# A graph layer on sorted edges: block bounds found by search and histogram, edge attributes kept column by column, one-hots shared with GpSimd

## The reference, cut to what matters

```python
def _L0_gnn_ref(x, edge_index, edge_attr, Wf1, bf1, Wf2, bf2, Wn1, bn1, Wn2, bn2):
    past, future = (edge_index[0], edge_index[1])
    x_p = x[past]
    x_f = x[future]
    flow_fwd = jnp.concatenate([x_f, x_p, edge_attr], axis=1)
    flow_bwd = jnp.concatenate([x_p, x_f, edge_attr], axis=1)
    flow_total_in = jnp.concatenate([flow_fwd, flow_bwd], axis=0)
    flow_processed = _mlp(flow_total_in, Wf1, bf1, Wf2, bf2)
    dest = jnp.concatenate([future, past], axis=0)
    flow_total = jax.ops.segment_sum(flow_processed, dest, num_segments=x.shape[0])
    return _mlp(flow_total, Wn1, bn1, Wn2, bn2)

def _L1_gnn_ref(x, edge_index):
    row, col = (edge_index[0], edge_index[1])
    return jax.ops.segment_sum(x[col], row, num_segments=x.shape[0])

h = jnp.maximum(_layernorm(x, axis=-1), 0.0)
x = x + _L0_gnn_ref(h, edge_index, edge_attr_16, ...)
h = jnp.maximum(_layernorm(x, axis=-1), 0.0)
x = x + _L1_gnn_ref(h, edge_index)
```

## Time and profile before

| | us |
|---|---|
| runs: median of 3 | 7755.75 |
| runs: lowest, highest | 7750.64, 7782.26 |
| profiled execution: span from first to last instruction | 7771.8 |
| busy: PE, weight loads, POOL, DVE, ACT | 5666.4, 4762.1, 4917.2, 3545.9, 1215.0 |

### The profile page before, as it was taken

One profiled execution on the slowest core, in us unless ns is written; L12 is line 12 of the kernel. 1 busy time (PEld: TensorE's weight loads), 2 busy tenths in 40 slices (PEclk: granted clock), 3 DMA queues, 4 the chain that ended last, 5 costly groups with the idle time before them and its releaser, 6 DMA issues.

```text
span 7771.8 us, 126735 instructions
## 1 busy us (share of the span) xinstructions
PE 5666.4 (73%) x26327; PEld 4762.1 (61%) x26328; DVE 3545.9 (46%) x15179; ACT 1215.0 (16%) x4039; POOL 4917.2 (63%) x4924
## 2 busy tenths in 40 slices
PE   2199999999999899999899998999943333333334
PEld 2077777777777777777777776888833333333334
DVE  8944444444444444444444444888833232232233
ACT  3211111111111111111111112333310000000000
POOL 0077777777777777777777775000037777777774
PEclk8566666666666766666666666555565555555555
DMA  5011111111111111111111112333211111111111
GB/s 130 5 41 41 41 41 41 41 40 41 41 40 40 40 40 41 40 40 40 41 40 40 40 40 52 68 70 70 60 16 14 14 14 14 14 14 14 14 14 17
DMA packets 1104013, 292.10 MB, mean 38 GB/s; under 512 B 1010042, under 2 KB 1052328, under 8 KB 1103553
## 3 DMA queue, kind: packets, MB, share of 16 engines
q1 hardware_dynamic: 947294, 102.88, 10.0%
q0 software_dynamic: 156672, 188.71, 9.8%
HBM read 226.56 MB, written 82.32 MB: 40 GB/s over the span
## 4 chain that ended last, share of the span: by engine, by line
POOL 54%; issue 27%; PE 11%; DVE 5%; DMA 2%; DVEq 1%; POOLq 0%; ACT 0%; ACTq 0%; SPq 0%
POOL t L518 19%; POOL records L486 18%; POOL g L476 17%; PE bank L782 4%; PE bank L732 1%; PE bank L731 1%; DVE acc L1007 1%; DVE oht L1076 1%; PE bank L730 1%; DVE ohd L1076 1%; PE bank L837 1%; DVEq L280 1%; DMA g<-t_rows,rec_i 1%; PE bank L758 0%; DMA t<-records 0%
## 5 line engine op out<-in xcount | busy, mean ns | idle before, releaser
L518 POOL DMA_INDIRECT t<-h_rows,didx x1568 | 1496.0, 954 | 1403.8 <-DMA didx<-records 925.9
L486 POOL DMA_INDIRECT records<-rec,pos x1664 | 1759.3, 1057 | 626.7 <-issue 451.3
L476 POOL DMA_INDIRECT g<-t_rows,rec_i x1664 | 1656.3, 995 | 756.0 <-issue 492.0
L837 PE MATMUL bank<-t,ohd 128*128 x1664 | 376.1, 402 | 1323.0 <-DMA t<-h_rows,didx 1323.0
L1016 DVE TENSOR_TENSOR prod<-bank,q_row 128x392 f32<-128x392 f32 x416 | 235.8, 567 | 2214.2 <-PE bank L747 2037.1
L730 PE MATMUL bank<-g,ident 128*128 128x128 f32 x3328 | 908.5, 367 | 379.3 <-DMA g<-t_rows,rec_i 378.2
L837 PEld LDWEIGHTS bank<-t,ohd 128*128 128x128 f32 x1664 | 362.9, 330 | 1335.8 <-issue 1335.8
L732 PE MATMUL bank<-t,oht 128*128 x3328 | 1113.4, 429 | 0.0
L731 PE MATMUL bank<-wee,eaT 17*128 17x128 f32 x3328 | 1101.7, 423 | 0.0
L730 PEld LDWEIGHTS bank<-g,ident 128*128 128x128 f32 x3328 | 723.4, 268 | 397.9 <-issue 396.2
L1007 DVE TENSOR_TENSOR t<-t,bank 128x32 f32 x1664 | 304.4, 183 | 1430.5 <-PE bank L837 1419.6
(11 more groups left out here) (180 smaller groups left out, 7327.8 us busy)
## 6 DMA issues: line engine op xcount, KB each, us to landing
t<-records SPq DMA_DIRECT2D x104, 536.0 KB, 4.2
rec_i<-by_d_sd SPq DMA_DIRECT2D x1664, 1.0 KB
eat<-by_d_ea SPq DMA_DIRECT2D x1664, 8.0 KB
g<-t_rows,rec_i POOLq DMA_INDIRECT x1664
records<-rec,pos POOLq DMA_INDIRECT x1664
t<-h_rows,didx POOLq DMA_INDIRECT x1568
by_d_ea<-in_ea SPq DMA_DIRECT2D x1, 12500.0 KB, 47.0
t_rows<-t2s SPq DMA_DIRECT2D x26, 256.0 KB, 2.2
```

Of the source, the lines that this page charges most:

```text
L476: nc.gpsimd.indirect_dma_start(out=g2[:, r, u, :], out_offset=None, in_=t2_rows, in_offset=bass.IndirectOffsetOnAxis(ap=rec_i[:, r, u, 0:1 ...
L486: nc.gpsimd.indirect_dma_start(out=records, out_offset=bass.IndirectOffsetOnAxis(ap=pos[:, r, u:u + 1].bitcast(U32), axis=0), in_=rec[:, r ...
L518: nc.gpsimd.indirect_dma_start(out=h2g[:, w * W + t, :], out_offset=None, in_=h2_rows, in_offset=bass.IndirectOffsetOnAxis(ap=didx[:, k, t ...
L837: ins = nc.tensor.matmul(s_bank[r][:, u * D:(u + 1) * D], s_oh[r][:, u, :], h2g[:, bass.ds(at[r * U + u], 1), :].rearrange("p a f -> p (a ...
```

## The change

Five edits.

1. **dst bounds by search.** The 98 counts of `dst` go. The first `dst` of each of the 125 rows is loaded (`first_i`), compared with the 99 block starts (`lt`), and PE sums that to the row in which each bound lies. POOL gathers these 99 rows by an indirect DMA, and one DVE instruction counts within them.
2. **src histogram on PE.** The 98 counts of `src` on DVE and ACT go. The block number is split in two digits (13 and 8 values), DVE makes one-hots of both in bf16 (42 instructions of 800 elements per row), and 200 matmuls accumulate the histogram in one PSUM region; three small DVE instructions and four small matmuls turn it into bounds.
3. **Order.** The one-hots, the flag for unsorted edges and the first DVE work on the edge list come ahead of the layer norm. PE makes the schedules between iterations of `tables` (now written out), in banks 6 and 7; the two products of the weights come ahead of them. POOL waits for `sched_done` 2 before its first gather (before: for the 46 counts of ACT).
4. **Edge attributes column-major.** The input is transposed on the host before the launch, `by_d_ea` is 16 rows of 202,112, and SP loads 16 x 128 pieces straight into `eaT`. The four transposes of `eat` and ACT's copy of them go. The copy inside HBM is cut in 8 parts: SP issues the first ahead of the tables, ACT the other 7 behind them; SP waits for these 7 at window 12.
5. **src stage.** One-hots of tiles 0 and 2 stay on DVE (now a tensor_scalar), those of tiles 1 and 3 go to POOL, which copies the row of indices first. PE waits for both.

The core of the diff (the fallback for unsorted edges, buffers and names are left out):

```diff
@@ sync
+            sp.dma_start(by_d_sd[0:E, :].rearrange("(p c) f -> p (c f)", p=1600),
+                         sd.rearrange("(p c) f -> p (c f)", p=1600)).then_inc(by_d_copied, 16)
...
-            for to, of in ((by_d_sd, sd), (by_d_ea, ea)):
...
+            to, of = ea_part(0)
+            sp.dma_start(to, of).then_inc(ea_copied, 16)
...
-                        sp.dma_start(eat[:, r, u, 0:EA], by_d_ea[bass.ds(at[u], P), :]).then_inc(ld_ea[r], 16)
-            rounds(sp, load_edges)
+                        sp.dma_start(eaT[1:EA + 1, r, u, :], by_d_ea[:, bass.ds(at[u], P)]).then_inc(ld_ea[r], 16)
+            load_edges(0, True, False)
+            span(sp, 1, EARLY, load_edges)
+            sp.wait_ge(ea_copied, 16 * (EA_PARTS + 1))
+            span(sp, EARLY, NI, load_edges)
@@ gpsimd
+            pool.wait_ge(viol_ready, 1)
+            pool.dma_start(viol_row[:, :], viol[:, 2:3]).then_inc(viol_in, 16)
...
+                pool.dma_start(first_i[:, :], by_d_sd[0:E, :].rearrange("(p c) k -> p c k", p=NP)[:, 0, 1:2]).then_inc(first_in, 16)
+            pool.wait_ge(row_ready, 1)
+            nc.gpsimd.indirect_dma_start(
+                out=rows, out_offset=None, in_=by_d_sd[0:E, :].rearrange("(p c) k -> p (c k)", p=NP),
+                in_offset=bass.IndirectOffsetOnAxis(ap=row_i[:, :].bitcast(U32), axis=0)).then_inc(rows_in, 16)
...
-            pool.wait_ge(cum_act, N_ACT)
+            pool.wait_ge(sched_done, 2)
...
+            def src_one_hots(i, first, last):
+                for w in range(SW):
+                    pool.wait_ge(src_rows_ready, i * SW + w + 1)
+                    nc.gpsimd.tensor_copy(src_row[:, w, :], pairs[:, bass.ds((i * SW + w) * W, W), 0]).then_inc(src_row_copied, 1)
+                    pool.wait_ge(src_row_copied, i * SW + w + 1)
+                    for r in range(R):
+                        if not (first and w == 0):
+                            pool.wait_ge(ssum_ready, (i * SW + w) * R + r + 1 - R)
+                        for u in POOL_HOT:
+                            ins = nc.gpsimd.tensor_scalar(s_oh[r][:, u, :], iota128[:, :], src_row[:, w, r * U + u:r * U + u + 1], None, ALU.is_equal)
+                        ins.then_inc(phot_ready, 1)
@@ scalar
-            def count_src(b, m, first):
...
+            for c in range(1, EA_PARTS):
+                to, of = ea_part(c)
+                act.dma_start(to, of).then_inc(ea_copied, 16)
...
-                nc.scalar.activation(eaT[:, r % 2, :, :].rearrange("p u n -> p (u n)"), pb[1][0:EA + 1, :], ACT.Copy).then_inc(oht_ready, 1)
@@ tensor
+            for m in range(2):
+                pe.wait_ge(hot_ready, m + 1)
+                for g in range(HC // 8):
+                    ins = nc.tensor.matmul(pb[7][0:DA * 8, 0:DB * 8], hot_a[m][:, g, :, :].rearrange("p a k -> p (a k)"), hot_b[m][:, :, g * 8:(g + 1) * 8],
+                                           start=m == 0 and g == 0, stop=m == 1 and g == HC // 8 - 1)
+            ins.then_inc(hist_ps, 1)
...
+            pe.wait_ge(start_ready, 1)
+            nc.tensor.matmul(pb[7][0:NB, 481:482], ident[0:NB + 1, 1:NB + 1], start_col[:, :], start=True, stop=True).then_inc(n_ready, 1)
+            tables(2, False, False)
+            tile_counts(1)
+            span(pe, 3, 5, tables)
+            schedule(1, 0)
+            tables(5, False, False)
+            schedule(1, 1)
...
-                pe.wait_ge(ld_ea[r], 16 * U * (i + 1))
-                for u in range(U):
-                    ins = nc.tensor.transpose(pb[1][0:EA + 1, u * P:(u + 1) * P], eat[:, r, u, :], ident[:, :])
...
+                        pe.wait_ge(phot_ready, v)
@@ vector
+            def digit_one_hots(m):
+                cols = slice(m * HC, (m + 1) * HC)
+                for a in range(DA):
+                    nc.vector.tensor_scalar(hot_a[m][:, :, a, :], digits[:, 0, cols].rearrange("p (g k) -> p g k", k=8), float(a), None, ALU.is_equal)
+                for b in range(DB):
+                    ins = nc.vector.tensor_scalar(hot_b[m][:, b, :], digits[:, 1, cols], float(b), None, ALU.is_equal)
+                ins.then_inc(hot_ready, 1)
...
-            def count(k, b0, b1, before_):
...
+            own.step(nc.vector.tensor_scalar(junk_d[0:NB + 1, :], rows.rearrange("p (c k) -> p c k", k=2)[:, :, 1], thr_col[:, 0:1], 0.0, ALU.is_lt, ALU.add,
+                                             accum_out=in_row[:, :]))
...
-                ins = nc.vector.tensor_tensor(s_oh[r][:, u, :], iota128[:, :], pairs[:, col, 0].broadcast_to([P, P]), ALU.is_equal)
-                if u == U - 1:
+                ins = nc.vector.tensor_scalar(s_oh[r][:, u, :], iota128[:, :], pairs[:, col, 0], None, ALU.is_equal)
+                if u == DVE_HOT[-1]:
```

More of the change, by code:

```diff
@@ new lines, in _ @@
+            tables(6, False, False)
+            schedule(1, 2)
+            tables(7, False, False)
+            schedule(1, 3)
+            pe.wait_ge(hexp_ready, 1)
+            nc.tensor.matmul(pb[7][0:NB, 483:484], hexp[:, :, :].rearrange("p a b -> p (a b)")[:, 0:NB], ones[0:DA * 8, 0:1],
+                             start=True, stop=True).then_inc(ncol_ps, 1)
+            tables(8, False, False)
+            pe.wait_ge(ncol_ready, 1)
+            nc.tensor.matmul(pb[7][:, 0:NB], ncol[:, 0:1].broadcast_to([NB, P]), before[0:NB, 0:NB], start=True, stop=True)
@@ new lines, in _ @@
+            nc.tensor.matmul(pb[7][0:NB, 480:481], before[0:NB, 0:NB], ncol[:, :], start=True, stop=True)
+            nc.tensor.matmul(pb[7][0:NB, 481:482], upto[0:NB, 0:NB], ncol[:, :], start=True, stop=True).then_inc(n_ready, 1)
+            tables(9, False, False)
+            tile_counts(0)
+            tables(10, False, False)
+            schedule(0, 0)
+            tables(11, False, False)
+            schedule(0, 1)
+            tables(12, False, True)
+            schedule(0, 2)
+            schedule(0, 3)
@@ L1089, in records_summed @@
                         later = (r + AHEAD) % R
[L1090 removed]
+                        rows_ = src_rows(*window) if window and later == 0 else None
                         for u in range(U):
```

434 lines of the change are left out of this document (271 added, 163 removed).

## The result

The changed kernel takes 7451.31 us (median, 7438.67 to 7465.21) against 7761.98 for the kernel before. The ratio is 0.9595, 95% interval 0.9577 to 0.9613: 4.05% faster, 311 us. The forecast was 7557, with a range from 7505. The sign was right and the size wrong: two fifths of the gain (126 of 311 us) came from a place where the prediction had zero.

A forecast was written before the change was run, and what follows sets the result against it. POOL's indirect DMAs were taken to bound the edge stage, behind a fixed prelude. Gains of 169 (prelude), 0 (edge stage) and 30 (src stage) made 199 us off the median 7755.75: 7557 us, range 7505 to 7660.

The forecast's parts named there:

- The failing step: Edge stage: POOL's instructions stay the same, so 416 rounds of 10.65 us stay, a gain of 0 us.
- Prelude: Until the first scatter: replacing the counts and reordering brings it to 217 us from 386.4, a gain of 169.
- The digit one-hots: Prelude on DVE: 42 one-hots at 0.58 us, 24.4 us in all, between bounds of 0.19 and 0.99 each.
- The tables with the schedules between: Prelude: 13 table iterations of 5.36 us take 70 us, and with the waits for schedules they end at 159.
- the wait for `hexp`: Prelude: waiting for DVE's `hexp` holds table iterations 8 to 12 for 6 us, between 0 and 13.
- The tail of the `src` schedule: Prelude: it takes 18.5 us as before, behind the tables, up to 178 us; the memset ends at 185.
- How the copies act: Prelude: issuing seven attribute copies holds ACT 39 us and delays its first-round work by 15 us, bounds 0 and 22.
- The sentence drawn from the Trainium skill: Prelude: SP's small index loads each wait behind a large copy packet, first scatter at about 224, 7 us later.
- src stage: Src stage: sharing one-hots between DVE and POOL removes PE's waits for DVE, a gain of 30 us, between -10 and 49.
- rival 3: Src stage: POOL one-hots over 0.83 us would bound it; 7667 us at worst, some 7610 with half; chance 0.08.
- Rivals 1 and 2: Edge stage: PE's clock stays at 1.2 GHz, 7836 us, chance 0.09; or is lost in part, 7605 to 7655, chance 0.10.

The follow-up runs named there:

- a_late: The changed kernel with ACT's seven attribute copies issued together behind its first window instead of ahead of it; 7457.18 us.
- a_alldve: The changed kernel with all src one-hots back on DVE and none on POOL; 7506.52 us.
- a_tp: The changed kernel with four unused transposes on PE and their copy on ACT put back each round, loads left new; 7556.27 us, ratio 0.9729 to before.
- b_stt: The kernel before with DVE's position offset as a scalar_tensor_tensor with a constant tile instead of a tensor_scalar; ratio 1.0002 to before.
- a_both: The changed kernel with three small DVE rows in PSUM and one attribute copy issued behind each of seven windows; 7418.20 us, ratio 0.9565 to before.
- a_ps: The changed kernel with three of DVE's small rows moved from SBUF to PSUM; 7444.21 us.
- a_spread: The changed kernel with ACT's seven attribute copies issued one behind each of its first seven windows; 7424.72 us, ratio 0.9554 to before.
- b_str: The kernel before with DVE's seven small rows laid out with a stride of two elements; ratio 1.0019 to before.
- b_ps: The kernel before with three of DVE's small rows moved from SBUF to PSUM; ratio 1.0012 to before.
- b_col: The kernel before with only the column-major edge attributes, without their transposes and ACT copy, the HBM copy in one piece; 7668.25 us, ratio 0.9865 to before.
- b_dup: The kernel before with DVE's first instruction on the position counts done twice each round; ratio 1.0110 to the kernel before of its own group.

## Why the prediction was wrong

- **The failing step** is "POOL's instructions are the same, so 416 x 10.65 stays: 0 us". The count was the same, the length was not. The prediction took 1.057 and 0.996 us for what an issue costs. They were means over short issues and long ones; the rows of the time line with 0.95 and 1.02 stood beside them. Work on DVE at the wrong phase makes the long ones, edit 4 moves the phase, and 126 us went: a round took 10.32 us (4292.2 / 416), where 10.65 was to stay. In the prediction's terms: with 0 replaced by 126, 7557 becomes 7431, within 20 us of the 7451 measured; the prelude's 10 less and the nodes' 24 more make up most of the rest.
- **Prelude**, -169 forecast, -179 measured. The digit one-hots were taken at 0.58 between bounds of 0.19 and 0.99; they are 0.28, which is 12.4 us less for 42. `h` came at 66.5 instead of 77. The tables with the schedules between took 80.6 us from there (forecast 82), the wait for `hexp` 5.6 of them (forecast 6). The tail of the `src` schedule was taken as 18.5 us behind the last table; it was 10, since its first steps run beside the last iterations. So the memset ended at 164.5, not 185. Half of that was given back: memset to first scatter was 42.5 us, not 31.8. Without the copies it is 18.3 - 1.5 = 16.8, so they cost 25.7 (26.8 by a_late), where 15 was taken and 22 was the upper bound. That the whole term came within 10 us is partly luck: the memset ended 20 us earlier than forecast, and 11 of them were lost behind it. Two rows were misread, without consequence: in the earlier trace rows the 2655 packets are those under 2 KB, and the raw edges are the other 125, of 12,800 bytes; and the 44.47 us are the issue of the padding held behind the copy, not of the copy itself.
- **How the copies act** was half right. They don't hold ACT (5 us of issue), they hold SyncE's loads. The sentence drawn from the Trainium skill, page "DMA: Bandwidth & Descriptors", section on queues and completion order, described this case better than the sum did: by it the small loads wait each behind large packets. The trace agrees in kind: from 162 to 182 us 191 packets of SyncE's queue started among 128 of the copies' large ones, and 839 in the 4 us behind the last of these.
- **src stage**, -30 forecast, -29.4 measured; a_alldve shows that the sharing does it (816.6 without). The price of a one-hot on POOL, taken from 0.29, is 0.62, still under the 0.83 at which rival 3 would begin.
- **Rivals 1 and 2**, on the clock, gave nothing: 0.66 instead of 0.68, and POOL waited 11 us for positions in 3700, less than before. With the four transposes back, a_tp has a clock of 0.70 where the changed kernel has 0.66, so taking them away did lower it, as the prediction read from the rows. That is at odds with the Trainium skill, page "TensorE: Matmul & The Clock Gate", Part 4, by which transposes don't bring the full clock. PE's slack covered the loss.
- **Nodes**, +24, is no effect of the change. PE's work there ran at a clock of 0.72 in the profile of before and at 0.50 in that of the changed kernel. Of the twelve other profiles outside the two later groups, b_stt has 95.7 us, a_both 94.0, a_ps and a_spread 110, and the other eight 122 to 124, b_str and b_ps, which are the kernel before in all but small rows, among them.

## What to carry to other kernels

Before a stage bound by one engine's issues is called fixed, compare the mean of its instructions with the shortest ones of the same kind in the time line. Here the difference was time held up that no view names as a wait, and a change on another engine removed it. The background copy cost 27 to 30 us wherever it was issued in one burst; in pieces smaller than the slack of a round, one to a window, it cost 6 us, less than that stage varies by from profile to profile.

## What the hardware showed that I had not expected

An indirect DMA on POOL ran up to 0.4 us longer, without any idle time in the records, according to where DVE was in its round; at a given phase the extra time is the same to within 0.1 us. The Trainium skill, page "SBUF — State Buffer", section on the two separate sides, says that DVE and GpSimd share a pair of ports, which one holds for its whole instruction while the other is blocked, and that DVE takes it for its two-port modes, or for two inputs in SBUF against an instruction of GpSimd that reads SBUF. The kind of effect agrees, and it goes both ways: DVE's position offset took 0.40 instead of 0.16 us late in an indirect DMA, and lost that with an input in PSUM. What holds POOL up doesn't follow from that sentence: the plain sum, with one input and as long as the product with two (0.56 us each, so with no sign of a faster mode), does it, and the product (0 long of 1029) and the four accumulating instructions don't. In the small group other forms, other strides and PSUM outputs changed nothing.

That the phase is the cause rests on the rule found in nine traces, the same in every kernel, and on a_tp and b_col, which moved it; the run made to move the phase by DVE alone (b_dup) gave no answer. What in DVE's small group holds POOL up stays open.
